# A fused image-transformer block on one core: slots and PSUM banks of the steps, turns, norms and projections dealt out anew

## What is computed

```python
y = patches @ W.T + b                       # 768 -> 192
h = layernorm(y) * ln_w + ln_b
q, k, v = split(layernorm(h) @ Wqkv.T)      # 12 heads of 16, each rounded and clipped
attn = fake_quant(q @ k.T / N)              # levels 0 to 7
o = fake_quant(attn @ v)
h = h + o @ Wproj.T + bproj
x_enc = layernorm(h) @ enc_w + enc_b
route = softmax(x_enc @ sw_w + sw_b)        # 8 experts, the best one is taken
t = gelu(layernorm(h) @ w1[best] + b1[best])
h = h + (t @ w2[best] + b2[best]) * max(route)
```

## Time and profile before

| | before |
|---|---|
| median of 3 runs | 1064.12 us (1060.9 to 1066.42) |
| profiled execution, device time | 1064.42 us |
| its span | 1062.6 us |
| PE busy | 939.1 us (88%) |
| DVE busy | 748.2 us (70%) |
| ACT busy | 704.2 us (66%) |
| POOL busy | 506.8 us (48%) |
| DMA | 49 GB/s mean |
| mean granted clock of PE | 0.963 |

### The profile page before, as it was taken

How to read it: one execution, slowest core, us unless ns; L and a number is a source line. 1 busy time by engine, 2 the same in 40 slices (tenths; PEclk the granted TensorE clock), 3 DMA queues, 4 the chain that set the end, 5 groups by cost and what they waited for, 6 DMA issues and landing times.

```text
span 1062.6 us, 24814 instructions
## 1 busy us (share of the span) xinstructions
PE 939.1 (88%) x8170; PEld 806.7 (76%) x8170; DVE 748.2 (70%) x2854; ACT 704.2 (66%) x1516; POOL 506.8 (48%) x890
## 2 busy tenths in 40 slices
PE   5778989999989998998889989998999999898878
PEld 4566777878877877787778877877788787777766
DVE  3677677687768668676776778667677767768562
ACT  1367767677767667676666767767676776667642
POOL 4434554536355453625636265463626545452323
PEclk9888999999999999999989999999999999999879
DMA  8121111212111111112112111111111111000000
GB/s 258 52 60 31 51 60 36 70 36 64 43 50 46 49 57 42 58 42 64 46 35 61 43 53 42 49 61 39 57 42 53 47 46 46 9 13 12 13 12 27
DMA packets 31332, 52.48 MB, mean 49 GB/s; under 512 B 4653, under 2 KB 17886, under 8 KB 31206
## 3 DMA queue, kind: packets, MB, share of 16 engines
q1 hardware_dynamic: 31206, 50.90, 15.7%
HBM read 41.25 MB, written 9.63 MB: 48 GB/s over the span
## 4 chain that ended last, share of the span: by engine, by line
PE 29%; DVE 10%; ACT 8%; issue 5%; POOL 1%; DVEq 0%; ACTq 0%; POOLq 0%
PE mixed_ps L768 6%; PE mixed_ps L778 6%; PE near_ps L637 4%; PE mixed_ps L628 4%; ACT relu L888 3%; PE near_ps L719 3%; PE scores_ps L699 2%; ACT hid L923 1%; PE turn_ps L650 1%; DVE st L1111 1%; DVE prob L1150 1%; DVE h L1212 1%; ACT o_a L911 1%; DVE k_b L1172 1%; ACT y L852 1%
## 5 line engine op out<-in xcount | busy, mean ns | idle before, releaser
L888 ACT ACTIVATE relu<-scores_ps,c_prob 98x784 uint16<-98x784 f32 x384 | 347.8, 906 | 137.9 <-PE scores_ps L699 126.1
L969 POOL TENSOR_TENSOR ve<-mv,const_sb 128x1 f32<-128x1 f32 x294 | 62.1, 211 | 469.6 <-DVE mv L1309 469.3
L637 PE MATMUL near_ps<-we,x_sb 128*128 128x192 f32 x1176 | 259.7, 344 | 14.1 <-DMA const_sb<-in_const 8.6
L637 PEld LDWEIGHTS near_ps<-we,x_sb 128*128 128x128 f32 x1176 | 200.2, 199 | 20.7 <-DMA const_sb<-in_const 8.6
L982 POOL TENSOR_TENSOR expd<-econst,below 128x8 f32<-128x8 f32 x98 | 166.3, 1699 | 32.9 <-DVE below L1239 32.9
L972 POOL TENSOR_TENSOR rs<-ve,const_sb 128x1 f32<-128x1 f32 x294 | 164.9, 561 | 23.2
L1150 DVE TENSOR_SCALAR prob<-relu 98x784 bf16<-98x784 uint16 x384 | 155.4, 405 | 9.3 <-ACT relu L888 0.7
L778 PE MATMUL mixed_ps<-w_sb,hid 128*128 128x192 f32 x784 | 149.6, 335 | 0.0
L778 PEld LDWEIGHTS mixed_ps<-w_sb,hid 128*128 128x128 f32 x784 | 128.8, 195 | 1.3
L923 ACT ACTIVATE hid<-mixed_ps,b_sb 128x384 f32<-128x384 f32 (+1 forms) x128 | 74.8, 584 | 53.1 <-PE mixed_ps L768 50.7
L1125 DVE TENSOR_SCALAR xn<-h,mv,rs 128x192 f32<-128x192 f32 x196 | 83.2, 425 | 23.6 <-POOL rs L972 23.0
(11 more groups left out here) (154 smaller groups left out, 2233.7 us busy)
## 6 DMA issues: line engine op xcount, KB each, us to landing
x_sb<-in_x SPq DMA_DIRECT2D x98, 384.0 KB, 3.0
out<-out_sb SPq DMA_DIRECT2D x98, 96.0 KB, 1.6
we<-in_tok_w SPq DMA_DIRECT2D x1, 576.0 KB, 4.1
w_sb<-in_w SPq DMA_DIRECT2D x1, 384.0 KB
hid<-in_w_qkv SPq DMA_DIRECT2D x1, 288.0 KB
hid<-in_w_qkv SPq DMA_DIRECT2D x2, 144.0 KB
hid<-in_w SPq DMA_DIRECT2D x1, 256.0 KB
hid<-in_w SPq DMA_DIRECT2D x2, 128.0 KB
```

The lines of the kernel that those rows point to most:

```text
L637: pe.matmul(dst, x_sb[:, tile % X_RING, j], we[:, j], start=j == 0, stop=False)
L888: act.activation(relu16[:, u % 2], scores_ps[0:KEYS, 2 * (u % VISIT):2 * (u % VISIT) + 2, 0:2 * SEQ], ACT.Relu, scale=c_prob[0:KEYS, :]).t ...
```

## The change

Only numbers in the slot and bank tables change; no instruction is added or left out, and all shapes stay. The core of the difference (left out are lines of the same kind in the tables of statistics and norms, and most of those for a group with seven tiles):

```diff
-EVAC1_7 = [1, 4, 6, 7, 10, 13, 16]
+EVAC1_7 = [1, 4, 5, 7, 9, 13, 16]
-JOIN1_6 = [3, 5, 8, 11, 14, 17]
+JOIN1_6 = [2, 6, 8, 11, 14, 17]
-BIAS1_6 = [4, 6, 9, 12, 15, 18]
+BIAS1_6 = [3, 6, 9, 12, 15, 18]
...
-STEP_AT = [17, 18, 21, 22, 23, 24, 25, 26, 28, 31]
-STEP_BANK = [0, 0, 1, 1, 1, 1, 0, 0, 1, 0]
+STEP_AT = [17, 18, 21, 22, 23, 24, 25, 27, 28, 31]
+STEP_BANK = [0, 0, 1, 1, 1, 1, 1, 0, 0, 0]
...
-TURN3_6 = [18, 20, 25, 26, 30, 32]
+TURN3_6 = [18, 20, 25, 29, 31, 32]
...
-ROUTE = [2, 10]
+ROUTE = [2, 11]
...
-UP = [6, 6, 8, 9, 14, 15, 16, 17]
+UP = [6, 6, 8, 9, 14, 15, 15, 17]
...
-PROJ_BANK_6 = [1, 1, 0, 0, 0, 1]
+PROJ_BANK_6 = [1, 1, 0, 0, 1, 1]
```

More of the change, by code:

```diff
@@ L124 @@
 H_RING = 2 * NT
-EMBED_SPAN_6 = [2, 2, 2, 2, 2, 2]
+EMBED_SPAN_6 = [2, 2, 2, 3, 2, 2]
 EMBED_SPAN_7 = [1, 2, 2, 1, 2, 2, 2]
@@ L130 @@
 EVAC1_6 = [1, 4, 7, 10, 13, 16]
-EVAC1_7 = [1, 4, 6, 7, 10, 13, 16]
-STATS1_6 = [2, 5, 8, 11, 14, 17]
-STATS1_7 = [2, 5, 7, 9, 11, 14, 17]
-JOIN1_6 = [3, 5, 8, 11, 14, 17]
+EVAC1_7 = [1, 4, 5, 7, 9, 13, 16]
+STATS1_6 = [2, 6, 8, 11, 14, 17]
+STATS1_7 = [2, 5, 7, 9, 10, 14, 17]
+JOIN1_6 = [2, 6, 8, 11, 14, 17]
 JOIN1_7 = [3, 5, 7, 9, 11, 14, 17]
-BIAS1_6 = [4, 6, 9, 12, 15, 18]
+BIAS1_6 = [3, 6, 9, 12, 15, 18]
 BIAS1_7 = [4, 6, 8, 10, 12, 15, 18]
-NORM1_6 = [4, 7, 9, 12, 15, 18]
+NORM1_6 = [4, 7, 10, 12, 16, 18]
 NORM1_7 = [4, 7, 8, 10, 12, 15, 18]
-STATS2_6 = [7, 9, 12, 14, 17, 20]
+STATS2_6 = [7, 9, 12, 14, 18, 20]
 STATS2_7 = [7, 9, 11, 13, 15, 17, 20]
-JOIN2_6 = [7, 9, 12, 14, 17, 20]
+JOIN2_6 = [7, 9, 12, 14, 18, 20]
 JOIN2_7 = [7, 9, 11, 13, 15, 17, 20]
-NORM2_6 = [8, 10, 13, 15, 18, 21]
+NORM2_6 = [8, 10, 14, 15, 18, 21]
 NORM2_7 = [8, 10, 12, 14, 16, 18, 21]
-TURN2_6 = [10, 12, 14, 16, 19, 23]
-TURN2_7 = [10, 11, 13, 15, 17, 19, 23]
+TURN2_6 = [10, 12, 15, 16, 19, 23]
+TURN2_7 = [10, 11, 13, 15, 17, 20, 23]
 STEP_KINDS = [("rows", 0, 0), ("rows", 1, 0), ("rows", 2, 0), ("values", 0), ("values", 1),
               ("rows", 0, 1), ("rows", 1, 1), ("rows", 2, 1), ("values", 2), ("values", 3)]
-STEP_AT = [17, 18, 21, 22, 23, 24, 25, 26, 28, 31]
-STEP_BANK = [0, 0, 1, 1, 1, 1, 0, 0, 1, 0]
+STEP_AT = [17, 18, 21, 22, 23, 24, 25, 27, 28, 31]
+STEP_BANK = [0, 0, 1, 1, 1, 1, 1, 0, 0, 0]
 ORDER = sorted(range(len(STEP_AT)), key=lambda n: STEP_AT[n])
@@ L176 @@
 PROJ_6 = [15, 16, 21, 22, 27, 29]
-PROJ_7 = [14, 16, 17, 21, 22, 27, 29]
-RESID_6 = [16, 17, 22, 23, 28, 30]
+PROJ_7 = [14, 16, 16, 21, 22, 27, 29]
+RESID_6 = [16, 17, 22, 23, 28, 29]
 RESID_7 = [15, 17, 18, 22, 23, 28, 30]
-JOIN3_6 = [16, 18, 22, 23, 28, 30]
-JOIN3_7 = [15, 18, 18, 22, 23, 28, 30]
-NORM3_6 = [17, 19, 23, 24, 29, 31]
+JOIN3_6 = [16, 18, 22, 24, 28, 30]
+JOIN3_7 = [15, 18, 18, 22, 23, 29, 30]
+NORM3_6 = [17, 19, 24, 25, 29, 31]
 NORM3_7 = [17, 19, 20, 23, 24, 29, 31]
-TURN3_6 = [18, 20, 25, 26, 30, 32]
+TURN3_6 = [18, 20, 25, 29, 31, 32]
 TURN3_7 = [18, 21, 22, 24, 26, 30, 32]
@@ L194 @@
 EXP_7 = [4, 5, 6, 7, 12, 13, 14]
-SUMEXP = [8, 17]
-UP = [6, 6, 8, 9, 14, 15, 16, 17]
+SUMEXP = [9, 17]
+UP = [6, 6, 8, 9, 14, 15, 15, 17]
 DOWN_6 = [10, 11, 12, 18, 19, 23]
-DOWN_7 = [10, 11, 12, 13, 18, 19, 23]
-PROJ_BANK_6 = [1, 1, 0, 0, 0, 1]
-PROJ_BANK_7 = [1, 1, 1, 0, 0, 0, 1]
+DOWN_7 = [10, 11, 13, 13, 17, 19, 23]
+PROJ_BANK_6 = [1, 1, 0, 0, 1, 1]
+PROJ_BANK_7 = [1, 1, 0, 0, 1, 0, 1]
 ROUTE_BANK = [1, 1]
```

## The result

| | change | before |
|---|---|---|
| median | 1000.25 us of 4 runs (999.09 to 1002.62) | 1064.34 us of 4 runs (1060.9 to 1066.42) |
| ratio | 0.9404, 95% interval 0.9373 to 0.9434 | |
| profiled execution, device time | 1000.83 us | 1064.42 us |
| its span | 999.0 us | 1062.6 us |

The account below looks back on a forecast made before the run. PE, busy 88%, was taken to be bound by four mixed-bank waits, 38.6 us. Terms of 2.9 us a pass over 13 passes (37.8 us) and 4.7 us of clock took 1064.4 to 1022 us, range 1005 to 1052.

Parts of the forecast that it names:

- (a): Slots 1 to 3: rows step moved to slot 3, bank 0, next projection to bank 1; gain 0.5 us a pass.
- (b): Slot 4's values step to bank 0: the projection behind its spread no longer waits for v; gain 1.17 us a pass.
- (c): Second half's route between first and second down covers DVE's finish; gain 0.68 us a pass.
- (d): Third up and the turn from slot 16 to 15: the projection's wait for gelu goes; gain 1.20 us a pass.
- (e): Rows step of slot 17 gets a new wait for the low part, uncovered by (d); -0.34 us a pass.
- (f): Four users follow closely in their banks with about 0.1 us to spare; one refill, -0.3 us a pass.
- Moved statistics, joins, norms and turns: These edits on DVE and POOL lie beside PE's work, both with idle time every few slots; costed at nothing.
- The clock: Falls of PE's clock to half in six passes cost 9.5 us; half of that, 4.7 us, taken as gain.
- Rival 1: Shorter idle spells end all clock falls; 1017 us; chance 0.25.
- Passes 8 and 9: Pass 8, with a group of seven tiles, given no gain; pass 9 given the regular 2.9 us.
- Rivals 2 to 4: Waits move on, 1054 us, chance 0.2; nothing measurable, 1060 to 1069, 0.1; slower by nb waiting on POOL, 1072, 0.1.
- rival 2: ACT's relu, copies and gelus set the time, PE only arrives sooner; 1054 us or some 1040 halfway; chance 0.2.

Follow-up runs that it names:

- e3_banks: Kernel before with only the step times, step banks and projection banks of (a) and (b): 1045.47 us, ratio 0.9825.
- e5_late_nb: The changed kernel with the join and nb of one's first tile back in slots 3 and 4: 1001.01 us, ratio 0.9404.
- e4_banks_nb: e3_banks with the join of one's first tile in slot 2 and its nb in slot 3, ahead of the choice: 1044.21 us, ratio 0.9809.
- e2_route: Kernel before with only the second half's route moved between the first and second down: 1048.66 us, ratio 0.9847.
- e1_up: Kernel before with only the third up in slot 15 and the turn of one's third tile with it: 1050.14 us, ratio 0.9848.
- e16_five: e14_four_turns with the residual slots (RESID_6) of the change: 1002.3 us, ratio 0.9407.
- e8_four: Kernel before with the edits of e1_up, e2_route and e4_banks_nb together: 1020.6 us, ratio 0.9587.
- e13_turns_only: Kernel before with only the turns of three's fourth and fifth tile moved to slots 5 and 7: 1061.62 us, ratio 0.9977.
- e14_four_turns: e8_four with the turns of three (TURN3_6) of the change: 1023.15 us, ratio 0.9629.
- e6_old7: The changed kernel with all seven-tile tables as before: 995.42 us, ratio 0.9349.

## Why the forecast was right and wrong

- **What bounds the kernel**: right. PE's waits for its mixed banks went, and the time with them. Against the forecast of 1022 us the profiled execution is 21 us faster. By the table above 19.7 of them are in the twelve passes, 5.8 at the end and 0.8 in pass 8; pass 9 and the start took 4.3 and 0.8 us more than forecast.
- **(a)** 0.5: half of it by itself (e3_banks, 0.25, with the wait of 0.20 for the choice that I had feared). With the turns moved, slots 2 to 4 gained 0.85.
- **(b)** 1.17: 0.9 gained at the projection, and 0.9 lost again at the second `up` (e3_banks). In the change, which moves the residual, slots 4 to 8 took 9.34 us instead of 10.20. The reason by nb was wrong (e5_late_nb, e4_banks_nb: 0.1 us).
- **(c)** 0.68: it was 1.0 (e2_route), undersized.
- **(d) and (e)** 0.86: 0.85 (e1_up), the sum by luck. The new wait of the step of slot 17 appeared neither in e1_up nor in the change.
- **(f)** -0.3: none of the four close followers waits in a regular pass of the change. Four hand-overs of which I reckoned with 0.1 us to spare all held, so the term was nothing.
- **"Moved statistics, joins, norms and turns ... I cost them at nothing"** is the step that failed. Together with the residual, which I left out of the list though the change moves it, they are worth 1.1 us (turns and residual, e16_five against e8_four) and 0.8 us (the rest) a pass, that is 1.9 of the 4.1. The priced terms by themselves gave 2.2 and not 2.9. Against the forecast, that makes for the twelve passes 1.9 x 12 = 22.8 us more than forecast, 0.7 x 12 = 8.4 less, and 5.3 more for the clock, the 19.7 above. I had reasoned from busy shares: DVE has idle time every few slots. What counts is when its residual stands in its list against the next user of the bank.
- **The clock**: half of the 9.5 us was taken; all of it went. Rival 1 was right there. The count of six left out the longer fall at the end of pass 8. The Trainium skill (TensorE: Matmul & The Clock Gate, "A second HAM failure mode: psum-queue depth-cycling") says that short idle spells between groups of products can make the clock swing. These runs agree: no fall in slot 6 in e3_banks, e4_banks_nb or the change, eight in e1_up, seven in e2_route. But they don't give a sharp line: e13_turns_only and e14_four_turns fell in two or three passes of twelve.
- **Passes 8 and 9**: no gain in 8 came out by size, 0.8, but by luck: the pass lost a fall of the clock that cost about 2.3 us and gained about 1.5 us of waits. Pass 9 got the regular gain in the forecast, because its `one` has six tiles. But its `two` and `three` are groups 8 and 7, whose projections and `down`s go by the tables for seven tiles, at which I had not looked, and it became 1.4 us longer. With the old slots it is 2.1 us shorter than before (61.07 us in e6_old7).
- **Rivals 2 to 4** did not come about. But waits that move on, rival 2's mechanism, were real in the partial kernels (0.9 us a pass in e3_banks), only at an `up` for a residual and not at the scores for a `relu`; the change moves the residual too.
- **What would show it**: the four waits were to be under 8 us (1.8), falls fewer than six (none), passes of about 57.5 us (56.3); the wait at slot 17 was to appear and didn't.

The low end of 1005 took only good ends of the priced terms. It gave no room for what the unpriced edits might bring, and those were more than half of the table rows that change.

## What to carry to other kernels

When a user of a shared buffer is moved, follow the buffer in both directions: whom it now waits for, and who waits for it, down to the instruction that empties it and the slot in which that one is issued. An edit of another engine's slot that looks like housekeeping can be what keeps the gain; price it by the next wait it prevents. Parts that gain nothing alone (the turns) may be worth their place beside another part, so test them on top of the rest as well as by themselves.
